# Expert layer of six, second pass: the routing weights come from the first pass by way of DRAM, and its router is left out

## What is computed

```python
h = rmsnorm(x, ln2_w)
t = h.reshape(-1, d)                                   # 4096 x 256
probs = jax.nn.softmax(t @ gate_w.T, axis=-1)          # 4096 x 16
topv, topi = jax.lax.top_k(probs, 6)
topv = topv / jnp.sum(topv, axis=-1, keepdims=True)
cw = jnp.zeros((T, 16)).at[jnp.arange(T)[:, None], topi].add(topv)
g = jnp.einsum('td,eid->eti', t, eg_w)                 # 16 experts, 176 wide
u = jnp.einsum('td,eid->eti', t, eu_w)
routed = jnp.einsum('eti,edi,te->td', silu(g) * u, ed_w, cw)
shared = silu(t @ sg_w.T) * (t @ su_w.T) @ sd_w.T      # 352 wide
out = x + (routed + shared).reshape(b, s, d)
```

## Time and profile before

| | |
|---|---|
| median of 3 runs | 4557.97 us (4550.22 to 4559.98) |
| the profiled execution: its own time | 4553.52 us |
| its span, first to last instruction | 4551.8 us |
| TensorE matmul busy | 4012.4 us, 88% of the span |
| VectorE, ScalarE, GpSimd busy | 2689.9, 2073.9, 913.3 us |
| mean granted TensorE clock | 0.937 |
| stage moe2a | about 2817 to 3334 us |
| stage moe2b | about 3336 to 3818 us |

### The profile page before, as it was taken

The page is one execution under the profiler, slowest core; times in us unless marked ns, Lnnn a source line. Parts: engine busy times, 40 slices in busy tenths (PEclk is TensorE's granted clock), DMA queues, the critical chain, the costliest instruction groups (busy, mean ns, idle before and its releaser), DMA issues. The chain is left out here.

```text
span 4551.8 us, 76151 instructions
## 1 busy us (share of the span) xinstructions
PE 4012.4 (88%) x25840; PEld 3344.1 (73%) x25840; DVE 2689.9 (59%) x6149; ACT 2073.9 (46%) x5350; POOL 913.3 (20%) x746
## 2 busy tenths in 40 slices
PE   7885999999898877999999996999979998887791
PEld 4554899999776765888888885888868886665771
DVE  6877989989576336555555554433343334776633
ACT  6884666666223434444444443333333333665140
POOL 1112332333001431000000000222222222000245
PEclk9997999999998987999999998999989998998595
DMA  2001000000001014111111112000010000001344
GB/s 68 14 15 44 1 1 0 0 0 1 26 21 45 0 61 137 38 39 40 38 38 40 40 38 74 18 5 10 6 59 11 9 6 24 12 12 31 98 135 130
DMA packets 118894, 157.39 MB, mean 35 GB/s; under 512 B 15856, under 2 KB 83280, under 8 KB 118224
## 3 DMA queue, kind: packets, MB, share of 16 engines
q1 hardware_dynamic: 111744, 135.01, 9.4%
q0 software_dynamic: 6864, 18.75, 1.5%
HBM read 126.59 MB, written 27.13 MB: 34 GB/s over the span
## 5 line engine op out<-in xcount | busy, mean ns | idle before, releaser
L1213 ACT ACTIVATE peer_tab<-peer_sims 128x128 f32<-128x128 f32 x1024 | 305.6, 393 | 0.0
L1220 POOL TENSOR_TENSOR peer_tab<-peer_sims 128x2048 f32<-128x2048 f32 x64 | 246.2, 3867 | 289.4 <-ACT peer_sims L1197 260.2
L1268 DVE SCALAR_TENSOR_TENSOR peer_tab<-peer_tab,peer_th 128x2048 f32<-128x2048 f32 x128 | 298.2, 2370 | 2.6 <-ACT peer_tab L1213 2.3
L1285 PE MATMUL bank<-ident,peer_tab 128*128 128x128 f32 x2048 | 247.9, 275 | 24.6 <-DVE peer_tab L1268 24.6
L1285 PEld LDWEIGHTS bank<-ident,peer_tab 128*128 128x128 f32 x2048 | 234.5, 142 | 37.9 <-DVE peer_tab L1268 25.4
L1335 PE MATMUL bank<-peer_wd,peer_hh 128*128 128x256 f32 x1024 | 242.0, 379 | 1.2 <-DVE peer_hh L1326 1.2
L1308 PE MATMUL bank<-peer_hT,peer_wg 128*128 128x256 f32 x1024 | 242.7, 380 | 0.0
L645 DVE TENSOR_TENSOR moe2a_b<-moe2a_a,bank 128x512 f32<-128x512 f32 x104 | 71.4, 687 | 271.1 <-PE bank L551 239.6
L633 POOL TENSOR_TENSOR moe2a_hh_lo<-moe2a_hh,moe2a_hh_hi 128x512 fp32r<-128x512 f32 x104 | 141.0, 1356 | 369.9 <-ACT moe2a_hh_hi L624 353.0
L1308 PEld LDWEIGHTS bank<-peer_hT,peer_wg 128*128 128x128 f32 x1024 | 195.2, 191 | 26.6
L645 DVE TENSOR_TENSOR moe2b_b<-moe2b_a,bank 128x512 f32<-128x512 f32 x96 | 65.9, 687 | 250.1 <-PE bank L551 219.6
(11 more groups left out here) (538 smaller groups left out, 11453.1 us busy)
## 6 DMA issues: line engine op xcount, KB each, us to landing
mha_wo<-mha_wo SPq DMA_DIRECT2D x128, 256.0 KB, 2.7
m_y_rows<-moe_y SPq DMA_DIRECT2D x79, 128.0 KB, 1.7
att_ctxT<-in_ctxT_dram SPq DMA_DIRECT2D x32, 256.0 KB, 2.6
lin_ctxT<-in_ctxT_dram SPq DMA_DIRECT2D x16, 256.0 KB, 2.7
mem_ctxT<-in_ctxT_dram SPq DMA_DIRECT2D x16, 256.0 KB, 2.7
mem_ctx<-in_ctx_dram SPq DMA_DIRECT2D x16, 256.0 KB, 3.2
mha_wo<-mem_wo_parts SPq DMA_DIRECT2D x1, 4096.0 KB, 13.5
t_scratch<-mha_hTf SPq DMA_DIRECT2D x8, 512.0 KB, 3.6
```

The source lines that it names most:

```text
L1213: i = nc.scalar.activation(tab[g][h][:, b * P:(b + 1) * P], sims[:, g, h, P:2 * P], ACT.Identity, bias=sims[:, g, h, b:b + 1])
L1220: nc.gpsimd.tensor_tensor(out=tab[g][h][:].rearrange("p (a b) -> p a b", b=P), in0=sims[:, g, h, P:2 * P].unsqueeze(1).broadcast_to([P, NB ...
L1268: nc.vector.scalar_tensor_tensor(out=tab[g][h][:], in0=tab[g][h][:], scalar=th[:, g, h:h + 1], in1=tab[g][h][:], op0=ALU.is_ge, op1=ALU.mu ...
L1285: i = nc.tensor.matmul(TB[n % 2][:, j * P:(j + 1) * P], tab[g][h][:, blk * P:(blk + 1) * P], core.ident[:], start=(j == 0 and h == 0), sto ...
```

## The change

Stage moe2a stores each tile's `cwT[:, par]` (128 x 512, 256 KB) to a new DRAM tensor `moe2_shares` from SP (`store_shares_sp`), and before ScalarE overwrites a buffer of `cwT` it also waits until that store has landed. Stage moe2b loads the tiles from there (`load_shares_sp`) instead of computing them: the router's matrix isn't loaded, and logits, softmax, selection of six, transposes, copies out of PSUM and low parts of the routing weights are not issued; TensorE waits ahead of its first CW matmul of a tile for the load. Both stages have four more semaphores.

```diff
@@ -164,7 +164,7 @@
             sp.dma_start(out, in_).then_inc(self.down_in, 16)
 
 
-def ffn_stage(core, name, kind, front_kind, blocks, top_k=0, first=0, store=False, inputs=None, inputs_loaded=False):
+def ffn_stage(core, name, kind, front_kind, blocks, top_k=0, first=0, store=False, inputs=None, inputs_loaded=False, shares_out=None, shares_in=None):
 
@@ -227,8 +227,9 @@
         cwTf, cwT_hi, cwT = sb("cwTf", [64, TILE]), sb("cwT_hi", [64, TILE], FP32R), sb("cwT", [P, 2, TILE], FP32R)
         e_ready, cw_done, cw_zeroed, cw_init, cwT_ready = sem("e_ready"), sem("cw_done"), sem("cw_zeroed"), sem("cw_init"), sem("cwT_ready")
         sel_zeroed = sem("sel_zeroed")
+        shares_stored, shares_loaded = ([sem(f"shares_{n}{i}") for i in range(2)] for n in ("stored", "loaded"))
         router_chain = Chain(sem("router_chain"), 9)
-        NF = NTR + 2
+        NF = NTR + (2 if shares_in is None else 0)
     if relu:
         bup, bdn = inputs.bup, inputs.bdn
         y_sum = sem("y_sum")
@@ -409,6 +410,8 @@
         act.wait_ge(f_filled, (t + 1) * NF)
         if some(t):
             act.wait_ge(cwT_ready, t)
+        if shares_out is not None and some(t - 1):
+            act.wait_ge(shares_stored[par], (t // 2) * 16)
         nc.scalar.activation(cwT[0:32, par, :], F[0:32, :], ACT.Copy)
         if isinstance(t, int) and t < 2:
             nc.scalar.activation(cwT[64:P, par, :], F[64:P, :], ACT.Copy)
@@ -594,8 +597,10 @@
             projected(U[j % 2][:], wus, par, j).then_inc(u_ready, 1)
             if some(n - 1):
                 pe.wait_ge(hh_ready, n - 1)
-            if j == 0:
+            if j == 0 and shares_in is None:
                 pe.wait_ge(cwT_ready, t + 1)
+            if j == 0 and shares_in is not None:
+                pe.wait_ge(shares_loaded[par], (t // 2 + 1) * 16)
             if is_first(t) and j % QB == 0:
                 pe.wait_ge(w_lo_made, (j // QB + 1) * (len(raws) - 1))
                 pe.wait_ge(w_hi_made, (j // QB + 1) * len(raws))
@@ -676,6 +681,15 @@
         dve.wait_ge(f_emptied, (t + 1) * NF)
         nc.vector.tensor_tensor(out=cwT[32:64, par, :], in0=cwTf[32:64, :], in1=cwT_hi[32:64, :], op=ALU.subtract).then_inc(cwT_ready, 1)
 
+    def store_shares_sp(sp, t, par):
+        sp.wait_ge(cwT_ready, t + 1)
+        sp.dma_start(shares_out[:, bass.ds(t * TILE, TILE)], cwT[:, par, :].bitcast(FP32)).then_inc(shares_stored[par], 16)
+
+    def load_shares_sp(sp, t, par):
+        if some(t - 1):
+            sp.wait_ge(cw_ready, (t - 1) * NB)
+        sp.dma_start(cwT[:, par, :].bitcast(FP32), shares_in[:, bass.ds(t * TILE, TILE)]).then_inc(shares_loaded[par], 16)
+
     def residual_dve(dve, t):
         dve.wait_ge(hh_used, (t + 1) * NB)
         xt = x[:, bass.ds(t * (GT * D), GT * D)]
@@ -703,13 +717,15 @@
              13: [(3, 2)], 14: [(3, 3)]}
     TURN = {4: 0, 8: 1, 11: 2, 15: 3}
 
+    routed = gated and shares_in is None
+
     def front_pe(pe, t, j):
 
         if ln and not peer and j == TRANS:
             transposes_pe(pe, t)
-        if gated and j == LOGITS:
+        if routed and j == LOGITS:
             logits_pe(pe, t)
-        if gated and j == WEIGHTS:
+        if routed and j == WEIGHTS:
             cwT_pe(pe, t)
         if peer and j in SCORES:
             scores_pe(pe, t, SCORES[j])
@@ -730,9 +746,9 @@
                 transposes_act(act, t, par)
             else:
                 loaded_act(act, t, par)
-        if gated and j == ROUTER:
+        if routed and j == ROUTER:
             router_act(act, t)
-        if gated and j == WEIGHTS:
+        if routed and j == WEIGHTS:
             cwT_act(act, t, par)
         if peer and j in SCORES:
             scores_act(act, t, SCORES[j])
@@ -750,10 +766,10 @@
     def front_dve(dve, t, par, j):
         if ln and not peer and j == NORM:
             norm_dve(dve, t)
-        if gated and j == ROUTER:
+        if routed and j == ROUTER:
             router_dve(dve, t)
         if split and j == LOW:
-            if gated:
+            if routed:
                 low_weights_dve(dve, t, par)
             low_dve(dve, t, par)
         if peer and j in PICK:
@@ -790,7 +806,7 @@
     QB = 4
     QUADS = -(-NB // QB)
     if gated:
-        loads = [(gw[:], args[name[:4] + "_gate"].rearrange("(c p) e -> p c e", p=P))]
+        loads = [] if shares_in is not None else [(gw[:], args[name[:4] + "_gate"].rearrange("(c p) e -> p c e", p=P))]
         raws = [sb(f"raw{n}", [P, QB * P]) for n in range(2 * C)] + [sb("raw_wd", [P, QB, D]), sb("raw_sel", [P, QB * P])]
         raw_in = [sem(f"raw_in{n}") for n in range(len(raws))]
         w_hi_made, w_lo_made = sem("w_hi_made"), sem("w_lo_made")
@@ -885,8 +901,21 @@
                 for quad in range(2, QUADS):
                     load_quad_sp(sp, quad)
             if not ln:
-                with sp.Fori(2, NT) as t:
-                    load_front_sp(sp, t)
+                if shares_in is not None:
+                    load_shares_sp(sp, 0, 0)
+                    load_shares_sp(sp, 1, 1)
+                with sp.Fori(1, NT // 2) as pair:
+                    for par in range(2):
+                        load_front_sp(sp, pair * 2 + par)
+                        if shares_out is not None:
+                            store_shares_sp(sp, pair * 2 + (par - 2), par)
+                        if shares_in is not None:
+                            load_shares_sp(sp, pair * 2 + par, par)
+                if shares_out is not None:
+                    for par in range(2):
+                        store_shares_sp(sp, NT - 2 + par, par)
+                    for par in range(2):
+                        sp.wait_ge(shares_stored[par], 16 * NT // 2)
             if store:
                 with sp.Fori(0, NT) as t:
                     sp.wait_ge(y_used, t + 1)
@@ -946,8 +975,9 @@
             if gated:
                 loaded_act(act, 0, 0)
                 split_act(act, 0, GATE_UP)
-                router_act(act, 0)
-                cwT_act(act, 0, 0)
+                if routed:
+                    router_act(act, 0)
+                    cwT_act(act, 0, 0)
                 split_act(act, 0, DOWN)
             else:
                 if relu:
@@ -980,8 +1010,9 @@
             if gated:
                 low_dve(dve, 0, 0)
                 split_dve(dve, 0, GATE_UP)
-                router_dve(dve, 0)
-                low_weights_dve(dve, 0, 0)
+                if routed:
+                    router_dve(dve, 0)
+                    low_weights_dve(dve, 0, 0)
                 split_dve(dve, 0, DOWN)
             else:
                 if relu:
@@ -4025,8 +4056,9 @@
         if 5 in stages:
             self_attention_stage(core, attention_inputs, 4 in stages, wo_rows)
             attention_inputs.close()
-            ffn_stage(core, "moe2a", "gated", "scratch", blocks=13, top_k=6)
-            ffn_stage(core, "moe2b", "gated", "scratch", blocks=12, top_k=6, first=13)
+            shares = nc.dram_tensor("moe2_shares", (P, T), FP32, kind="Internal").ap()
+            ffn_stage(core, "moe2a", "gated", "scratch", blocks=13, top_k=6, shares_out=shares)
+            ffn_stage(core, "moe2b", "gated", "scratch", blocks=12, top_k=6, first=13, shares_in=shares)
         if 6 in stages:
             head_attention_stage(core, "att32", quant=False)
         if 7 in stages:
```

## The result

The changed kernel takes 4531.23 us (median, 4523.36 at the least), the kernel before 4557.97. The ratio is 0.9945 with an interval of 0.9933 to 0.9957: 25 us faster (20 to 31). The prediction was 4532 in a range of 4523 to 4541. One execution of the changed kernel (5280.8 us) and one of the kernel before (4812.04) lie far above the rest and are left out of the ratio.

The account below looks back on a forecast made before the run. TensorE was taken to bound moe2b. Gains of 21.7 (tiles), 1.6 (tile 0) and 3.0 (start) less 0.5 (clearing) gave 25.8 us off the 4557.97 median: 4532 us, range 4523 to 4541.

Parts of the forecast that it names:

- Tiles 2 to 7's fronts: moe2b, beside tiles 1 to 6: router work and its waits vanish, every block takes 4.426 us, gaining 21.7 us.
- the tile without a front: Last tile of moe2b: ten blocks at 4.426 us each set the bare pace, 53.11 us for 12 blocks.
- The slow subtraction: moe2b tiles: GpSimd's subtraction took 2.32 us in place of 1.28 beside VectorE's low part of tokens; nothing taken as remaining.
- the page's rule: Skill page: VectorE instructions with two SBUF inputs contend with GpSimd; 0.3 us a tile could stay, 2 us less gain.
- Tile 0: moe2b's first tile: removing the logits gains nothing, a 1.9 us wait replaces them; the rest of the front gains 1.6 us.
- The start: Start of moe2b: down weights split 7.3 us earlier, but the first routing-weight load holds TensorE; gain 3.0 us.
- the restart: Start of moe2b: 12 projection matmuls of block 1 run after idleness, nine at 0.43 us and three at 0.23.
- The added work: Stores in moe2a and loads in moe2b are hidden; clearing eight more semaphores costs 0.5 us.
- (a): moe2b: only TensorE's own work goes, waits set by other engines stay; gain 16.5 us, 4541.5 us; 7%.
- (b): Start of moe2b gives nothing or costs, the load queueing 4 us longer; gain 21.8 us, 4536 us; 8%.
- (c): moe2a: stores hold ScalarE's copies and TensorE stops; kernel 10 us slower, 4568 us; 1%.
- (d): moe2b: TensorE without pauses gets a lower clock; six slow blocks eat the gain, eight give 4568 us; 2%.

Follow-up runs that it names:

- The experiment with the weights' part kept: Changed kernel, but VectorE still makes one 32 x 512 subtraction ahead of the tokens' low part in moe2b, result unused: 4525.29 us.
- The repeats: Changed kernel and the kernels with VectorE's 32 x 512 subtraction or the VectorE and ScalarE router work kept, each run once more: 4523.75, 4532.64 and 4531.65 us.
- the three executions with the long block: Changed kernel with TensorE's front work, the other engines' router work, or only VectorE's 32 x 512 subtraction kept: block 1 of tile 0 took 6.51, 6.58, 6.95 us.
- the repeat: The changed kernel run once more with nothing but a blank line added: 4523.75 us.
- the kept parts: Changed kernel with TensorE's logits and transposes still issued, 4540.24 us; changed kernel with VectorE's and ScalarE's router work still issued, 4535.75 us.
- the stores alone: Changed kernel with moe2a's stores, but moe2b runs its own router and loads nothing: 4551.56 us, against 4541.83 for the kernel before.

## Why the prediction was right

**Tiles 2 to 7's fronts.** 21.7 was forecast, 21.65 measured. The parts bear it out, not the sum alone: 13.57 of TensorE's own work against 6 x (1.70 + 0.35 + 0.1 + 0.1) = 13.5, and 7.65 for the waits and the slow subtraction, for which 21.7 - 13.5 = 8.2 were left. The argument that carried it was the one from the tile without a front: what is between 53.11 and 56.73 belongs to the front, whatever its chain.

**The slow subtraction.** It was taken as nothing because the overlap would shrink to about 0.5 us and GpSimd had 0.9 to spare; it shrank to 0.34 and cost 0.19. The experiment with the weights' part kept shows that the spare time, and not the absence of contention, is the reason: at 1.16 us of overlap GpSimd loses 1.02 and the block pays 0.27, so the spare time is 0.75 rather than 0.9. The 2 us that the page's rule could have left stayed away, though the rule itself holds.

**Tile 0.** 1.6 forecast; from block 3 to tile 1 it takes 3410.11 - 3368.25 = 41.86 instead of 3418.14 - 3374.66 = 43.48, 1.62 less. The wait left was sized at 1.9 and is 1.56; the block that holds it is 6.44 - 4.43 = 2.01 longer, as the sum had it (3.6 - 1.6). That the logits gained nothing there is borne out by the kernel that kept them.

**The start.** 3.0 forecast, 3.34 measured, and the steps are right one by one, counted from the stage's first instruction: raw_wd of quad 2 at 18.4, measured 18.26; the load issued at 19.3, measured 19.24; landing 5.0, measured 5.1; CW of block 0 at 24.3, measured 24.41. The one term that was off is the restart: nine of twelve matmuls were put at 1.2 GHz, and the stretch from CW of block 0 to CW of block 1 took 3362.17 - 3357.74 = 4.43 where 4.9 was taken. The repeats show that this term is not a constant: block 1 took from 5.50 to 6.95. That the start's gain lies so near to 3.0 (3.34, in the repeat 3.22) is therefore in part luck: in the three executions with the long block, where the wait for the load also ended 0.5 to 1.3 us later, block 3 began at 36.88 to 37.28, a gain of 1.0 to 1.4. A forecast of it to better than some 2 us isn't to be had from one trace. The 2.6 us for the load that the prediction quotes from the Trainium skill (DMA: Bandwidth & Descriptors, "Anatomy of one DMA") stand there for transfers that GpSimd issues; SP's six loads by themselves took 2.7 to 2.8, and the first one, right behind quad 2, took 5.1, which is what the prediction went by.

**The added work.** Stores and loads are hidden as forecast, with 4.3 and 2.7 us against some 50 (the 48 us taken for a store are those of a tile of 12 blocks; moe2a has 13, and 54 were measured). Clearing costs 0.52 for eight semaphores (0.5 forecast).

**The rest.** From tile 7 to the next stage 61.20 instead of 61.34. So 21.65 + 1.62 + 3.34 + 0.14 = 26.75, the stage's whole gain, with the clearing behind moe2b inside the last term. In the repeat it is 21.64 + 1.63 + 3.22 - 1.10 = 25.39: the last term is the low clock behind the stage's last wait, which the same kernel showed once and not the other time. moe2a is 0.77 longer: 0.27 is the clearing, the other 0.5 lies within what moe2a differs by among kernels that are alike there (518.00 to 520.28).

**The rivals.** (a) falls by the kept parts; (b) had its mechanism, a queue of TensorE that stands for the load, but the load landed in 5.1 and not 4 us later; (c) falls by the stores alone; (d) by the clock of 1.00 in the tiles. What the prediction didn't see is how much lay beside the change: the wait for the load could be moved away, and behind it the split of whole quads ahead of one block, in both stages.

## What to carry to other kernels

Where one iteration of a loop runs without a side task, the difference of the iterations is the price of that task, and it holds even if some of it is waits on other engines; keep each half of the task once to see that they add up. When a computed operand becomes a loaded one, the load's place in the issuing queue decides the start, so put it by when it is first needed and not behind prefetches. After such a wait is gone look at what else stands in one piece ahead of the first iterations (here the split of a quad): spreading it was worth about half as much as the change.
